# Who copies the V projections out of their PSUM bank: ScalarE in place of DVE, in a fused cross-attention kernel

## What is computed

```python
q = (x   @ Wq.T + bq)   # 8 batches, 224 queries, 512 features -> 16 heads of 32
k = (ctx @ Wk.T + bk)   # 8 batches, 750 keys
v = (ctx @ Wv.T + bv)
att = softmax(q k^T / sqrt(32))          # per head
out = (att v) @ Wo.T + bo
out = layernorm(x + out) * gamma + beta
```

## Time and profile before

| | us |
|---|---|
| median of 3 executions (639.09 to 639.73) | 639.18 |
| the profiled execution, its own time | 640.04 |
| its span, first to last instruction | 637.3 |
| PE / DVE / ACT / POOL busy | 611.6 / 501.1 / 352.5 / 468.0 |

### The profile page before, as it was taken

One profiled execution on the slowest core, in us unless ns is written; L12 is line 12 of the kernel. 1 busy time (PEld: TensorE's weight loads), 2 busy tenths in 40 slices (PEclk: granted clock), 3 DMA queues, 4 the chain that ended last, 5 costly groups with the idle time before them and its releaser, 6 DMA issues.

```text
span 637.3 us, 13655 instructions
## 1 busy us (share of the span) xinstructions
PE 611.6 (96%) x5217; PEld 425.4 (67%) x5217; DVE 501.1 (79%) x680; ACT 352.5 (55%) x673; POOL 468.0 (73%) x459
## 2 busy tenths in 40 slices
PE   8998999999999999999999999999999999899894
PEld 7766677766676676766677676766767666576542
DVE  4677787788797797887787887977878887757885
ACT  4514566556565465664665565664656656444661
POOL 9633677784987589784987759785897869775853
PEclk9999999999999999999999999999999999899998
DMA  9574532562245523754137532564237422421020
GB/s 304 186 183 126 133 78 72 133 145 70 65 110 142 129 63 89 151 127 125 38 86 167 143 77 62 115 147 118 69 88 169 96 62 51 107 69 25 2 59 29
DMA packets 95776, 67.02 MB, mean 105 GB/s; under 512 B 69780, under 2 KB 81760, under 8 KB 95712
## 3 DMA queue, kind: packets, MB, share of 16 engines
q1 hardware_dynamic: 95200, 65.41, 41.2%
q0 software_dynamic: 512, 0.75, 0.5%
HBM read 24.52 MB, written 3.67 MB: 44 GB/s over the span
## 4 chain that ended last, share of the span: by engine, by line
PE 69%; POOL 14%; DVE 12%; issue 3%; DMA 1%; ACT 1%; POOLq 0%; SPq 0%; DVEq 0%; ACTq 0%
PE ps_task L610 34%; PE ps_scores L626 10%; PE ps_scoresT L650 8%; PE ps_task L666 6%; POOL pair_sums L1036 6%; DVE top L928 4%; PE ps_task L564 4%; POOL head_sums L1041 3%; DVE token_parts L905 3%; POOL head_sums L1044 3%; PE ps_scores L610 2%; POOL rstd L1056 2%; PE ps_task L692 2%; DVE attn_sums L935 1%; DMA x_in<-in_x 1%
## 5 line engine op out<-in xcount | busy, mean ns | idle before, releaser
L809 ACT ACTIVATE probsT<-ps_scoresT 125x448 f32<-125x448 f32 x384 | 204.5, 544 | 154.2 <-PE ps_scoresT L650 148.4
L928 DVE TENSOR_REDUCE top<-ps_scores 112x1 f32<-112x750 f32 x256 | 234.2, 927 | 63.8 <-PE ps_scores L626 63.0
L1036 POOL TENSOR_TENSOR pair_sums<-probsT 125x672 f32<-125x672 f32 x122 | 197.8, 1621 | 72.3 <-ACT probsT L809 65.6
L650 PE MATMUL ps_scoresT<-stacks 100*125 100x224 f16 x768 | 135.8, 261 | 1.5 <-ACT probsT L809 1.2
L610 PE MATMUL ps_task<-wvT,ctxT 128*125 128x512 f16 x564 | 135.6, 379 | 0.1
L610 PE MATMUL ps_task<-ctxT,wkT 128*128 128x375 f16 x708 | 130.7, 323 | 0.0
L626 PE MATMUL ps_scores<-stacks 96*112 96x512 f16 (+1 forms) x512 | 125.6, 327 | 4.8 <-DVE top L928 4.0
L650 PEld LDWEIGHTS ps_scoresT<-stacks 100*125 100x125 f16 x768 | 94.5, 137 | 41.2 <-ACT probsT L809 4.9
L1041 POOL TENSOR_TENSOR head_sums<-pair_sums 125x224 f32<-125x224 f32 x122 | 96.6, 792 | 11.4
L610 PEld LDWEIGHTS ps_task<-wvT,ctxT 128*125 128x125 f16 x564 | 73.2, 136 | 33.1 <-DVE parts L885 0.4
L1044 POOL TENSOR_TENSOR head_sums<-head_sums,pair_sums 125x224 f32<-125x224 f32 x122 | 87.3, 715 | 9.6
(11 more groups left out here) (103 smaller groups left out, 533.7 us busy)
## 6 DMA issues: line engine op xcount, KB each, us to landing
stacks<-parts SPq DMA_DIRECT2D x248, 60.9 KB, 2.0
ctx_in<-in_ctx SPq DMA_DIRECT2D x8, 768.0 KB, 5.5
stacks<-parts SPq DMA_DIRECT2D x124, 46.9 KB, 2.0
resid<-in_x SPq DMA_DIRECT2D x8, 448.0 KB, 4.1
ctx_in<-in_ctx SPq DMA_DIRECT2D x7, 512.0 KB
out_y<-y SPq DMA_DIRECT2D x16, 224.0 KB, 2.3
x_in<-in_x SPq DMA_DIRECT2D x8, 256.0 KB, 3.1
stacks<-parts SPq DMA_DIRECT2D x124, 14.0 KB, 1.8
```

The source lines that it names most:

```text
L650: last = nc.tensor.matmul(ps_scoresT[0:KP, piece % 2, NQ * i:NQ * i + NQ], stacks[:, g, h, KP * k:KP * k + KP], stacks[:, g, h, Qc], start ...
L809: nc.scalar.activation(probsT[0:KP, g % 2, h, 2 * j:2 * j + 2, :].rearrange("p k q -> p (k q)"), ps_scoresT[0:KP, piece % 2, 0:2 * NQ], AC ...
L928: nc.vector.tensor_reduce(top[0:QP, g % 2, HG * q + h:HG * q + h + 1], ps_scores[0:QP, s % RING, 0:NK], AX.X, ALU.max).then_inc(top_ready, 1)
L1036: nc.gpsimd.tensor_tensor(pair_sums[0:KP], probsT[0:KP, g % 2, h, 0:3, :], probsT[0:KP, g % 2, h, 3:6, :], ALU.add).then_inc(pair_sums_rea ...
```

## The change

ScalarE's `high_part` gets the V tasks of the iterations, first thing in the step after the task; it counts a semaphore of its own, `v_saved`. DVE no longer copies them. It still has to count `task_saved`, which must rise in the order of the tasks, so behind its row maximum it waits for `v_saved` and for its own last count and adds one. The two V copies of the prologue stay on DVE.

```diff
+                if t[0] == "V":
+                    nc.scalar.copy(v[parity][0:KP, t[1]], bank[0:KP, :]).then_inc(v_saved, 1)
+                    return
...
-                        t, n, _, bank, _, _ = saved
-                        high_part(t, n, bank)
+                        t, n, _, bank, _, of_next = saved
+                        high_part(t, n, bank, 1 - parity if of_next and s else parity, True)
...
+                elif v_copied is not None:
+                    dve.wait_ge(v_saved, v_copied)
+                    dve.wait_ge(task_saved, n)
+                    dve.sem_inc(task_saved, 1)
...
-                    if saved is not None and saved[0][0] == "V":
-                        t, n, splits, bank, batch, of_next = saved
-                        save_task(t, n, splits, bank, batch, 1 - parity if of_next and s else parity)
                     if has_step(b, s + 1):
                         row_max((s + 1) % STEPS, T + 1, UNITS * b + (s + 1) // UNIT)
                     if has_output(b) and s - 2 in O_STEPS:
                         mean_of(O_STEPS.index(s - 2))
-                    if saved is not None and saved[0][0] != "V":
+                    if saved is not None:
                         t, n, splits, bank, batch, of_next = saved
-                        save_task(t, n, splits, bank, batch, parity)
+                        v_copied = None if t[0] != "V" else v_copies(b, s)
+                        save_task(t, n, splits, bank, batch, parity, v_copied)
```

More of the change, by code:

```diff
@@ L280, in build @@
         maxima_saved, probs_ready, attn_copied = sem("maxima_saved"), sem("probs_ready"), sem("attn_copied")
-        high_saved, attn_high_saved = sem("high_saved"), sem("attn_high_saved")
+        high_saved, attn_high_saved, v_saved = sem("high_saved"), sem("attn_high_saved"), sem("v_saved")
         top_ready, task_saved = sem("top_ready"), sem("task_saved")
@@ L773, in _, with high_part @@
         def _(act):
-            def high_part(t, n, bank):
-                if t[0] not in SPLIT_KINDS:
+            def high_part(t, n, bank, parity=0, copy_v=False):
+                if t[0] == "O" or t[0] == "V" and not copy_v:
                     return
                 act.wait_ge(task_ready, n + 1)
+                if t[0] == "V":
+                    nc.scalar.copy(v[parity][0:KP, t[1]], bank[0:KP, :]).then_inc(v_saved, 1)
+                    return
                 dst, src, b16 = split_views(t, bank, 0)
@@ L874, in _, with save_task @@
         def _(dve):
-            def save_task(t, n, splits, bank, batch, parity):
+            def save_task(t, n, splits, bank, batch, parity, v_copied=None):
                 kind = t[0]
@@ L965, in _, with v_copies @@
             row_max(0, 0, 0)
+            def v_copies(b, s):
+                done = sum(t[0] == "V" for at, t in tasks_of(b).items() if at < s)
+                return sum(t[0] == "V" for i in range(b) for t in tasks_of(i).values()) + done
             def iteration(b, parity):
```

## The result

The changed kernel takes 642.46 us (median of 8 runs, 641.09 to 643.37) beside 639.13 us for the kernel before in the same session (8 runs, 637.48 to 639.73): a ratio of 1.0061, 95% interval 1.0048 to 1.0073. It is 0.6% slower; 642.1 was forecast. Its profiled execution took 642.8 us with a span of 640.3 us, 3.0 us longer than the span of before.

A forecast was written before the change was run, and what follows sets the result against it. PE, busy 96% of the span, was taken to bound the kernel. V5's copy, 2.8 us, plus DVE's count, 0.1, gave +2.9 us on 639.18: 642.1 us, range 640.4 to 644.0.

The forecast's parts named there:

- V5's copy: At step 10 of iterations 0 to 6, ScalarE's copy delays casts and then PE by 0.40 us each: 2.8 us.
- The other five copies: V0 to V4 of each iteration on ScalarE cost 0; without cover by idle time or a half task, 0.4 us each.
- DVE's count: DVE's added wait for ScalarE delays PE's output projection after V2 in iteration 7: +0.1 us, or +0.55 if it must wait.
- DVE's relief: 31.8 us leaving DVE gains 0, 0.2 us as a bound; as a rival for faster, 4%, 636.2 us if all came back.
- The 0.03 us: At step 14 the scores' weight load begins 0.03 us behind PE's K half, held by the row maximum.
- The signs: Profile signs: step 10's `token_low` 2.00 us behind the exponential, PE's maxima waits 4.0 to some 7 us, DVE 32 us less busy.
- The clock: Rival, 13% in two halves: a second dip in iteration 0, 643.7 us (8%); the dip at 548 gone, 640.5 (5%).

The follow-up runs named there:

- e1: Changed kernel with V5's copy alone back on DVE, ahead of its row maximum; the other 38 copies stay on ScalarE: 638.23 us, ratio 0.9999 to the kernel before.
- e2: Changed kernel with only V5 copied by ScalarE, the other V tasks by DVE as before: 641.91 us, ratio 1.0057 to the kernel before.
- e4: Changed kernel with V5's copy on ScalarE behind the casts of step 10, DVE's count behind its `token_low`: 638.09 us, ratio 1.0000 to the kernel before.
- e5: Changed kernel with a second 125x512 ScalarE operation, the bank copied onto itself, directly behind V5's copy: 646.88 us, ratio 1.0124 to the kernel before.
- e6: Kernel before (V copies on DVE) with the third split of step 10 put into step 11: 637.92 us, ratio 0.9985 to the kernel before.
- e9: Changed kernel (V copies on ScalarE) with the three splits spread over steps 9, 10 and 11: 636.49 us, ratio 0.9963 to the kernel before.
- e3: Changed kernel with V5 of iteration 0 alone copied by DVE: 640.92 us, ratio 1.0046 to the kernel before.
- e0: The changed kernel once more, with no edit: 642.23 us beside 638.49 for the kernel before, ratio 1.0054.
- e7: Changed kernel (V copies on ScalarE) with the third split of step 10 put into step 11: 637.83 us, ratio 0.9989 to the kernel before.
- e8: Kernel before (V copies on DVE) with the three splits spread over steps 9, 10 and 11: 635.88 us, ratio 0.9955 to the kernel before.

## Why the prediction was right, point by point

- **V5's copy, 7 x 0.40 = 2.8 us.** Right, and shown from four sides: with V5 back on DVE the loss is gone (e1), with V5 alone moved it is all there (e2), behind the casts the copy is free (e4), and a second one adds its slot (e5). Measured 0.39 to 0.41 us in each of iterations 1 to 6, and 0.42 in iteration 0 of e2, where no dip hides it: 2.8 us in sum. The copy takes 0.584 us where 0.60 was taken, and its slot is 204.41 - 203.97 = 0.44 us for the exponential and 203.97 - 203.51 = 0.46 for the copy, where 0.43 and 0.49 were used.
- **The other five copies, 0.** Right: no shift at any of their steps, in the changed kernel or in e1.
- **DVE's count, +0.1 us.** It cost nothing measurable. In iteration 7 of the changed kernel:

```profile
586.32 0.59 ACT L780 COPY v<-ps_task 125x512 f32<-125x512 f32 x1 [0.75 <-PE ps_task L610]
...
586.64 1.78 DVE L935 TENSOR_REDUCE top<-ps_scores 112x1 f32<-112x750 f32 x2 [1.58 <-PE ps_scores L626]
...
587.05 2.34 PEld L564 LDWEIGHTS ps_task<-woT,attn_parts 128*112 128x112 f16 x12 [0.28 <-DVEq L894]
```

  PE goes on 0.73 us after the copy's start; before it was 0.74. The first of the two row maxima runs from 586.64 to past 587.5, so the count at about 587.0 passed while it ran. The rule of the Trainium skill cited in the prediction (PSUM — Partial Sum Buffer, engine and sequencer instructions) agrees. The +0.1 us had no row behind it, and no run shows it.
- **DVE's relief, 0.** Right in what it is worth, off in its size: 27.3 us of busy time went, not 31.8. The row maxima grew by 1.1 us (234.2 to 235.3); the rest I put, without a run for it, to the overlap in time between a copy's end and the next operation's start (0.69 us long, 0.61 from start to start in the earlier trace rows, about 0.08 us each), which busy time counts once. The 0.03 us by which the chain was read to end behind PE was rather 0.08, by e6 to e9; e4, where DVE is rid of V5's copy and PE isn't delayed, got none of it back. The Trainium skill's advice on offloading (Perfetto Trace Analysis, Optimizing Scalar/DVE Operations) speaks of a saturated DVE, and so isn't tested here: DVE went from 79% to 74% and the time up by 0.6%.
- **The signs.** `token_low` 2.00 us behind the exponential and a wait of over 0.26 us: as forecast. PE's wait for maxima rose to 5.8 us, not to some 7, because part of the delay is entered at the weight loads (their waits for issue went from 18.7 to 21.1 us). One step failed: I had the 1.5 us wait of iteration 0 grow to 1.9. It stayed at 1.48, and the time came two operations earlier, in the wait for an exponential that ScalarE now makes later:

```profile
61.08 0.41 PE L650 MATMUL ps_scoresT<-stacks 100*125 100x224 f16 x2 [1.00 <-ACT probsT L812]
...
63.91 0.84 PE L626 MATMUL ps_scores<-stacks 96*112 96x512 f16 x2 [1.48 <-DVE top L935]
```

  Without V5 on ScalarE in iteration 0 (e3) the first of these waits is 0.51 us. I had followed one chain, while the copy delays both engines' inputs by the same 0.4 us; the sum isn't touched.
- **The clock.** Both halves of that rival happened in one profile, at +1.4 and -1.6 us. The dip in iteration 0 appeared in three of the four profiles with V5's copy ahead of all three casts there (the changed kernel, e0, e5, but not e2), and in none of the eight others. The dip near 548 us was in the profiles of before, e5 (later, by what its shifts add), e7 and e8. It was missing in e1 and e4 among others, which run PE's work at the same distances as before, and e2 has one near 614 us instead (0.56 and 0.58 in two windows).

  Each run also comes with its mean granted clock, in which the end of the kernel counts too: behind PE's last matmul every profile falls to 0.50. Of the twelve profiles, the five without a dip ahead of that have a mean of 0.996 or 0.997, the six with one dip 0.993 to 0.995, and e5 with two has 0.991. Read so, 50 of the 69 runs of before that stood beside the experiments met no dip, at a median span of 635.9 us, but only 5 of the 14 runs of the changed kernel and e0, at 639.2: 3.3 us apart. If runs at 0.997 alone are taken on both sides (8 of before, 636.4), it is 2.8 us. So the spans without a dip put the loss at 2.8 to 3.3 us, and the 2.8 of the copies rests on the shifts. Where up to 0.5 us above that comes from stays open; the start-up alone differed between the profiles by -0.4 to +0.7 us from that of before. The more frequent dips lift the medians further (3.3 us above before for the changed kernel, 3.7 for e0; 2.4 for e3 with its six steps), so that the median of 642.46 lies so near the forecast 642.1 is partly luck. That the changed kernel meets the lower clock more often is measured; what decides in which execution it falls stays open, and no experiment aimed at it.

## What to carry to other kernels

When an operation moves to a less busy engine, don't ask how busy that engine is but what stands behind the new place in its list, and whether the last of that is waited for with no slack: here 0.58 us of work with three casts behind it cost 0.41 us an iteration, and the same work three casts later nothing. Time freed on an engine that waits for the bounding one was worth nothing, as e1 and e9 show. And a chain that the bounding engine waits for is the place to edit first: spreading its three splits over three steps gave 0.45%, more than any assignment of the copies, most of it in iteration 0, where PE had stood 1.5 us at the end of the chain. Finally, medians can hide a loss when runs at two clocks mix in them, as in e6 and e7; the distances between marks in the traces show it.

## What the runs showed of the hardware

`token_low`, a DVE operation with two SBUF inputs, has a length that goes with what GpSimd does meanwhile. In the changed kernel the three of step 10 take 1719, 1142 and 1146 ns, behind each other and beside GpSimd's sums; the last of e7, in a pause of GpSimd (205.91 to 206.84 us), takes 0.68 us. In the profile of before, 14 of the 56 run while GpSimd does nothing, and all of them take 0.68 or 0.69 us. In e9's iteration 0, spread over three steps:

```profile
55.95 0.69 DVE L912 TENSOR_TENSOR token_parts<-ctx_in,token_parts 128x512 f16<-128x512 f32 x1 [1.28 <-ACT token_parts L796]
...
58.36 1.70 DVE L912 TENSOR_TENSOR token_parts<-ctx_in,token_parts 128x512 f16<-128x512 f32 x1 [0.74 <-ACT token_parts L796]
...
61.43 0.68 DVE L912 TENSOR_TENSOR token_parts<-ctx_in,token_parts 112x512 f16<-112x512 f32 x1
```

The first of these falls into a pause, the second runs beside GpSimd's sums (from 57.90 us on). The third starts 0.02 us ahead of GpSimd's next sum (61.45) and is short as well, so being beside a sum is not enough to make one long, and what decides stays open. Part of what the spreading wins is therefore probably that two of the three are short. The other surprise was the count: an increment on DVE's queue passed while the row maximum ahead of it was still running, so here a count placed behind a long instruction didn't wait for its end.
